# Attention of a GNN kernel: the score products of a unit are spread between the transposes of its exponentials

## The reference, cut to what matters

```
q = (z @ Wq + bq).reshape(L, H, D);  k = ...;  v = ...        # L = 512, H = 8, D = 64
scores = einsum('ehd,ehd->eh', q[row], k[col]) / sqrt(D) + bias
p = exp(scores - segment_max(scores, row)[row])
alpha = p / segment_sum(p, row)[row]
out = segment_sum(alpha[:, :, None] * v[col], row).reshape(L, C) @ Wo + bo
```

## Time and profile before

| | |
|---|---|
| median of 3 executions | 394.52 us (393.35 to 395.64) |
| the profiled execution | 393.12 us, of which the span from first to last instruction is 391.6 us |
| granted TensorE clock | 0.999 on average |
| TensorE products (PE) / weight loads (PEld) | 371.8 / 277.1 us busy |
| VectorE (DVE) / ScalarE (ACT) | 307.4 / 168.8 us busy |
| the attention's units | about 112.5 to 177 us of the span |

### The profile page before, as it was taken

One profiled execution on the slowest core, in us unless ns is written; L12 is line 12 of the kernel. 1 busy time (PEld: TensorE's weight loads), 2 busy tenths in 40 slices (PEclk: granted clock), 3 DMA queues, 4 the chain that ended last, 5 costly groups with the idle time before them and its releaser, 6 DMA issues.

```text
span 391.6 us, 5047 instructions
## 1 busy us (share of the span) xinstructions
PE 371.8 (95%) x1772; PEld 277.1 (71%) x1772; DVE 307.4 (78%) x659; ACT 168.8 (43%) x281; POOL 5.3 (1%) x25
## 2 busy tenths in 40 slices
PE   4999799999999999999999999999999999999994
PEld 2465455566657888887678788887588878787873
DVE  5878998999858789896877977599875777498346
ACT  5453576483124243244569533262364521135320
POOL 5000000000000000000000000000000000000000
PEclk9999999999999999999999999999999999999999
DMA  6602444353135000067300412300510041000002
GB/s 230 262 0 55 125 153 158 126 165 114 49 101 195 2 2 2 2 214 291 140 3 0 142 74 59 155 2 1 172 44 0 0 143 74 0 2 0 0 7 102
DMA packets 16360, 32.92 MB, mean 84 GB/s; under 512 B 1360, under 2 KB 1488, under 8 KB 16336
## 3 DMA queue, kind: packets, MB, share of 16 engines
q1 hardware_dynamic: 15744, 32.25, 23.8%
q10 hardware_dynamic: 592, 0.36, 0.3%
HBM read 21.07 MB, written 1.05 MB: 56 GB/s over the span
## 4 chain that ended last, share of the span: by engine, by line
PE 73%; DVE 13%; ACT 5%; DMA 4%; issue 3%; ACTq 1%; SPq 1%; DVEq 0%
PE acc L1482 8%; PE bank L1464 8%; PE bank L1575 7%; PE bank L1338 6%; PE bank L1339 6%; PE bank L1319 4%; PE acc L1319 4%; PE acc L1339 4%; PE acc L1338 4%; PE bank L1560 3%; PE acc L1546 3%; DMA big<-z_sb 2%; DVE big_rounded L675 2%; PE acc L1296 2%; PE bank L1296 2%
## 5 line engine op out<-in xcount | busy, mean ns | idle before, releaser
L1482 PE MATMUL acc<-wide_rounded,c_rounded 128*126 128x512 f32 x168 | 50.3, 439 | 2.5 <-ACT acc L511 2.5
L1482 PEld LDWEIGHTS acc<-wide_rounded,c_rounded 128*126 128x126 f32 x168 | 30.7, 186 | 19.7 <-issue 14.1
L815 DVE TENSOR_SCALAR wide_rounded<-iota_f,picked 128x512 fp32r<-128x512 f32 x84 | 36.0, 480 | 2.9 <-PE acc L1482 2.9
L506 ACT COPY z_sb<-acc 126x512 f32<-126x512 f32 x37 | 21.6, 585 | 35.7 <-PE acc L1482 21.9
L530 ACT ACTIVATE wide<-wide,low_col 128x512 f32<-128x512 f32 x32 | 21.3, 716 | 32.9 <-DVE low_col L973 32.8
L1575 PEld LDWEIGHTS bank<-v_sb,big 128*128 128x128 f32 x256 | 29.7, 192 | 4.7 <-issue 4.3
L648 DVE TENSOR_TENSOR wslot_rounded<-wslot,wide_rounded 128x512 fp32r<-128x512 f32 x24 | 16.2, 688 | 21.3 <-ACT wslot L416 21.3
L1575 PE MATMUL bank<-v_sb,big 128*128 128x65 f32 x256 | 31.6, 277 | 0.0
L1464 PE MATMUL bank<-t_sb,wslot 128*128 128x512 f32 x64 | 29.3, 593 | 0.7 <-DVE t_sb L904 0.7
L675 DVE TENSOR_TENSOR big_rounded<-big,big_rounded 128x1024 fp32r<-128x1024 f32 x24 | 29.1, 1222 | 0.5
L821 DVE TENSOR_TENSOR c_rounded<-row_bc,wslot_rounded 128x1008 fp32r<-128x1008 bf16 x21 | 25.2, 1201 | 0.1
(11 more groups left out here) (338 smaller groups left out, 779.1 us busy)
## 6 DMA issues: line engine op xcount, KB each, us to landing
big<-z_sb SPq DMA_DIRECT2D x36, 252.0 KB
big<-in_w SPq DMA_DIRECT2D x4, 2048.0 KB, 7.9
x_sb<-in_x SPq DMA_DIRECT2D x8, 256.0 KB, 4.8
big<-in_w_3t SPq DMA_DIRECT2D x2, 1024.0 KB, 7.2
row_bc<-in_rows SPq DMA_DIRECT2D x7, 256.0 KB, 6.6
wslot<-in_wq SPq DMA_DIRECT2D x1, 1024.0 KB, 8.5
wslot<-in_wk SPq DMA_DIRECT2D x1, 1024.0 KB, 10.4
wslot<-in_wv SPq DMA_DIRECT2D x1, 1024.0 KB, 12.4
```

Of the source, the lines that this page charges most:

```text
L506: nc.scalar.copy(stage[0:BROWS, b % STAGES, :], a).then_inc(S["staged"], 1)
L815: nc.vector.tensor_scalar(hot_ring[:, u, k, :], iota_f[:, :], picked[:, 0, s0 + k:s0 + k + 1], None, ALU.is_equal)
L1482: last = nc.tensor.matmul(to, st_ring[:, u, 2 * k + a, :, :].rearrange("p w k -> p (w k)"), hot_ring[:, u, k, :], start=False, stop=False, ...
```

## The change

Before, the loop over n runs all 8 transposes of T(n), then all 6 products of S(n + 2), then W(n - 1). After, for n = 1 to 13, T(n) is cut in four quarters of two transposes, and after each of the first three comes one pair of S(n + 2). The last quarter is followed by W(n - 1). The waits are the same, at the same instructions. For n = 0, 14 and 15 the order is as before. Nothing is computed differently, and no other engine's order changes.

```
             def scores(n):
-                m, k = n // 4, n % 4
-                if n >= 2:
-                    pe.wait_ge(S["lows_found"], 2 * n - 2)
-                for i, (left, right) in enumerate(((q_hi, k_hi), (q_hi, k_lo), (q_lo, k_hi))):
-                    for a in range(2): ...
+                for i in range(3):
+                    score_part(n, i)          # one pair of products; i == 0 waits for lows_found
+            def e_turn_part(n, quarter):
+                a, half = quarter // 2, quarter % 2
+                i = 2 * n + a
+                if half == 0:
                     pe.wait_ge(S["e_ready"], i + 1)
                     if i >= 2:
                         pe.wait_ge(S["p_ready"], i - 1)
-                    for t in range(NT):
+                for t in (2 * half, 2 * half + 1):
                     last = nc.tensor.transpose(tile(bank[4 + a], t), tile(held_e[:, i % HELD, :], t), ident[:, :])
+                if half == 1:
                     last.then_inc(S["e_turned"], 1)
...
             for n in range(UNITS + 1):
-                if n < UNITS:
-                    e_turn(n)
+                for quarter in range(4 if n < UNITS else 0):
+                    e_turn_part(n, quarter)
+                    if 1 <= n < UNITS - 2 and quarter < 3:
+                        score_part(n + 2, quarter)
...
-                if n + 2 < UNITS:
-                    scores(n + 2)
+                if n == 0:
+                    scores(2)
                 if n >= 1:
                     weighted(n - 1)
```

More of the change, by code:

```diff
@@ L1536, in _, with score_part @@
                 chunk_weights(j + 1, late_slots)
-            def scores(n):
-                m, k = n // 4, n % 4
-                if n >= 2:
-                    pe.wait_ge(S["lows_found"], 2 * n - 2)
-                for i, (left, right) in enumerate(((q_hi, k_hi), (q_hi, k_lo), (q_lo, k_hi))):
[L1544 to L1553, removed]
+            def score_part(n, i):
+                m, k = n // 4, n % 4
+                left, right = ((q_hi, k_hi), (q_hi, k_lo), (q_lo, k_hi))[i]
+                if n >= 2 and i == 0:
+                    pe.wait_ge(S["lows_found"], 2 * n - 2)
+                for a in range(2):
+                    r = slice(a * DH, (a + 1) * DH)
+                    last = nc.tensor.matmul(bank[2 * (n % 2) + a][:, :], left[r, k, m * P:(m + 1) * P],
+                                            right[r, k, :], start=(i == 0), stop=(i == 2))
+                if i == 2:
+                    last.then_inc(S["st_mm"], 1)
+            def scores(n):
+                for i in range(3):
[4 more added lines that the diff above has]
+                if half == 0:
                     pe.wait_ge(S["e_ready"], i + 1)
@@ L1558, in e_turn @@
                         pe.wait_ge(S["p_ready"], i - 1)
-                    for t in range(NT):
-                        last = nc.tensor.transpose(tile(bank[4 + a], t), tile(held_e[:, i % HELD, :], t), ident[:, :])
+                for t in (2 * half, 2 * half + 1):
+                    last = nc.tensor.transpose(tile(bank[4 + a], t), tile(held_e[:, i % HELD, :], t), ident[:, :])
+                if half == 1:
                     last.then_inc(S["e_turned"], 1)
```

## The result

| | before | after |
|---|---|---|
| time, median | 394.06 us (4 runs, 393.35 to 395.64) | 401.62 us (4 runs, 400.99 to 402.54) |
| profiled execution, span | 391.6 us | 401.1 us |
| first load of T(1) to first load of T(15) | 120.38 to 172.27: 51.89 us | 120.92 to 180.13: 59.21 us |
| a unit of the steady part | 3.70 us (some 3.79) | 4.35 us |

The changed kernel is slower: 1.0203 times the time before, 95% interval 1.018 to 1.0225, that is 8.0 us more (7.1 to 8.9); the two medians lie 7.6 us apart. The attention alone, between the two marks of the table, grew by 7.3 us.

A forecast was written before the change was run, and what follows sets the result against it. TensorE was taken to bound units 1 to 13; 10.4 us for added row changes, less 0.7 (last unit) and 0.3 (second-head waits), gave +9.4 on 393.8, so 403.2 us, range 399.5 to 406.5.

The forecast's parts named there:

- The bound: Units 1 to 13 of the attention: TensorE sets the pace, 3.70 us a unit before and 4.50 after.
- What costs: Edges between 64 and 128 rows: four more changes a unit at 0.20 us, 0.80 a unit, 10.4 us in 13 units.
- The way in: From T's last load to S's first: 0.31 us instead of a step of 0.11, then 0.11 of open load.
- 0.11 for a load in the open: At each change of rows, a weight load not covered by running products costs 0.11 us, beside 0.09 of drain.
- T's step: From one transpose load to the next in a group of two transposes and a pair: 0.11 us of 0.85.
- The last unit's share: Last of the 13 units: TensorE's idle time before the last T leaves only 0.07 of 0.80 us showing, minus 0.7.
- The waits for the second head: T's loads taking 0.99 instead of 0.91 us, waiting for the second head's exponential, go in some units: minus 0.3 us.
- VectorE's `weigh`: Behind T, it waits 0.8 us for its second head every other unit; at 3.8 us a unit VectorE stays under 4.5.
- One sign of the prediction: End of the attention: if the forecast is right, the last T no longer waits for VectorE.
- Weights hidden under the other kind's products: Rival: S pairs cover transposes' loads, a unit is 3.3 us, VectorE bounds at 3.40; 4 us less, 390; 4 in 100.
- Partly covered: Rival at the edges of S: the drain costs, the open load does not; +3 to +5 us, 397 to 399; 6 in 100.
- VectorE taking over: Rival: `weigh`'s 0.8 us wait in seven units comes into the chain; +15 us, 409; 4 in 100.

The follow-up runs named there:

- 128-row kernels: Old order (kernel before) and new order (changed kernel), each score product taking all 128 partitions instead of one head's 64: 1.0071 and 1.0081 of the kernel before.
- unit 13 alone: Against the changed kernel, the interleaved order in unit 13 only, all other units as before: 394.47 us, one run.
- the scores of two units together: Against the kernel before, the score products of two units stand together after the transposes of each odd unit: 0.9967 of its time.
- the order T, W, S: Against the kernel before, scores(n + 2) stands behind weighted(n - 1) instead of ahead of it: 0.9953 of its time.

## Why the prediction was right, and where its size was off

- **The bound.** The prediction had TensorE alone in the chain through units 1 to 13: so it stayed.
- **What costs.** Each change between 64 and 128 rows of the array, by a drain and a load in the open, not the waits. The 128-row kernels show it: with the change of rows gone, the gaps go, and the orders cost the same. The way in is 0.20 us, as predicted, and "issue" stands before S's loads in 39 places instead of 13, three times as many, as predicted too.
- **The term that was mis-sized** is "0.11 for a load in the open" on the way out of S into transposes. It was read from S's own first pair (0.50 against 0.40) and carried over to T. The steps showed 0.06 there: behind S, T's second load comes 0.06 after the first, where the sum has 0.11 for "T's step". Why a transpose is held up less than a score product was not tried. So the second and third group took 0.80 us instead of 0.85, the last two transposes 0.16 instead of 0.22, a unit 4.35 instead of 4.50, and 13 such units would be 8.4 us, not 10.4. A row of the prediction held the hint: at 172.27, after an idle stretch, four loads of T took 0.42 us, while four at a step of 0.11 would take 0.47.
- **What comes off.** The last unit's share (0.65) was taken up whole by TensorE's idle time before T(15), as unit 13 alone shows: T(13) to T(15) is 7.12 us before and there, 7.11 in the changed kernel. The waits for the second head went. 12 x 0.65 less the 0.4 or so of waits is 7.4, against 7.3 measured. Their size was right and their reason was not: the prediction laid them on the second head's exponential, which ends at 146.42, but the fifth load of that T comes at 146.98 (146.40 plus 0.72 less 0.14), 0.12 behind the end of `weigh`'s second product (145.58 plus 1.28 is 146.86). It was `p_ready`, the same wait with the same 0.12 as in the kernel with the scores of two units together. In the slower units VectorE is done earlier, so either reason lets the wait go.
- **VectorE's `weigh`** did wait for T: between 125 and 175 us (engine, line, waited for: us in total, times, longest)

```profile
PEld bank L1567 <- issue: 8.2, 34, 0.2
DVE big L985 <- PE bank L1567: 6.4, 9, 0.9
...
PEld acc L1546 <- issue: 5.7, 34, 0.2
```

  In every second unit, six in all, it waited 0.7 to 0.9 us for the second head, as predicted (0.8). In three of them it also waited for the first head, 0.25 to 0.85 us, which the prediction did not have. Neither came into the chain: VectorE has 13.8 us of work in 17.4. One sign of the prediction did not come: the last T still waits for VectorE (weight loads of W(13), `weigh`, T(15)):

```profile
178.25 1.86 PEld L1583 LDWEIGHTS bank<-v_sb,big 128*128 128x128 f32 x16
...
179.33 1.28 DVE L985 TENSOR_TENSOR big<-bank,big 128x512 f32<-128x512 f32 x2
...
180.13 0.42 PEld L1567 LDWEIGHTS bank<-ident,wide 128*128 128x128 f32 x4
```

  W's first load and its usual 1.73 us would allow T(15) at 179.98. `weigh`'s first product ends at 180.01 (179.33 plus 0.68), and T's load follows it by 0.12, as elsewhere: 180.13.

- **The rivals.** Weights hidden under the other kind's products: no load of T begins before the streaming of a pair of S has ended (147.37 plus 0.11 for the load and 0.23 for the pair is 147.71, the load of T comes at 147.79), and even where nothing drains (128 rows) the new order is no faster. Partly covered: its size was 3 to 5 us and the forecast's 9.4, measured were 7.3, so the forecast was nearer; what was smaller was the load of one kind, not the cover of both. VectorE taking over: not seen.
- The time, 401.6 us, is 1.6 us under the forecast of 403.2: about 2 us less for the attention (7.3 against 9.4), of which the load in the open is 12 x 0.15 = 1.8. That 403.2 came within 1.6 us of the time is thus no luck of errors that cancel: one term was too large, and the others held in size.

## What to carry to other kernels

Count the changes between sub-array products (64 rows) and full ones, not the products: in this attention each cost 0.15 us on the way into transposes and 0.20 at every other edge, with or without a wait there, so products of the narrow kind belong together, as many as the banks and the consumers' latency allow. Before packing a queue more densely, ask what releases the slower engine's next task: with the product that VectorE waits for moved ahead, the stage's end came 0.9 us earlier, more than the cheaper edge gave in all units (0.6). And measure the open load of each kind at its own edge: it held up the work behind it for 0.06 us in one and 0.11 in the other.

## What the runs showed of the hardware that had not been expected

- A weight load of an fp32 transpose in the open delays the next step by 0.06 us, that of a rounded fp32 score product by 0.11 (0.49 to 0.50 us recorded, against 0.39 with the load covered), both of 128 columns. The Trainium skill, "TensorE: Matmul & The Clock Gate", LDWEIGHTS, gives columns divided by 1.2 as the time of a load in ns, 107 for 128 columns: if a load held up the next step for the whole of its time, both would be 0.11. The score products agree, the transposes do not, and for them the measurement decides. Whether a transpose's load is shorter or the work behind it starts before it is done was not tried.
- The way from 128 to 64 rows costs the same behind W as behind T: in the order T, W, S the score loads follow W's last load by 0.26 us, where another full load would follow by 0.06.
